# Moving a level-by-level update into places of its own, and running the levels in two groups

## The chip, the cores and the metric

The kernel runs on one core of one Trainium2 chip. The metric is the time of one execution on the device in microseconds (us); the profile comes from one execution of its own. TensorE (PE) multiplies matrices, VectorE (DVE) and ScalarE (ACT) work elementwise, GpSimd (POOL) does a few passes and powers, and SyncE (SP) issues the transfers. Each engine has a queue of instructions in a fixed order and they meet at semaphores. PSUM has eight banks, into which TensorE writes.

## The reference

Two layers run over 2,048 tokens of 256 channels (two sequences of 1,024). Layer 0 is an RWKV block: token shift, five mixed inputs made by a low-rank product, receptance, key, value, gate, a decay of its own for each channel and token, and the recurrence below, then a norm over each head, a gate, an output product; its feed-forward keeps the two largest of four hidden units. Layer 1 is a state-space block and a second feed-forward.

```python
def step(S, inp):                      # one token, each head
    r_t, k_t, v_t, d_t = inp
    kv = k_t[..., :, None] * v_t[..., None, :]
    y = jnp.einsum('bhj,bhji->bhi', r_t, S + u[None, :, :, None] * kv)
    return (d_t[..., None] * S + kv, y)
...
y = (y - mean_of_head) / sqrt(var_of_head + EPS)     # then gamma, beta, times silu(gate)
```

The products of the two branches are multiplied, a SiLU of the feed-forward with the output of the attention, and added to the input.

## The kernel before, in words

The tokens go through in tiles of T = 256. `rounds` calls `one(a, b)` on every engine: `a` is the tile that is in layer 0, `b` the one before it, in layer 1. A first round has only `a`, seven rounds have both (six of them in a hardware loop, one written out), and the last round has only `b`. So the work of two tiles is interleaved by hand in the lists at the end of each engine's `one`. `FILLS` gives for each PSUM bank the names that fill it in turn; `open_bank` waits until the name before was freed, `close_bank` says that a name is filled, `free` is the reader's answer.

**The recurrence** is turned into products. In a tile each pair of blocks of 1, 2, 4, 8, 16, 32 and 64 tokens (`LEVELS`) is a level: the keys of the earlier block, multiplied by the decay up to its end, meet the queries of the later block, multiplied by the decay since its start. `level_update` (L924) multiplies in place, half of `kT` and half of `rT` for each level, so a level can't be multiplied before TensorE has read the level before. TensorE does `own_products` (the tokens with themselves, with the bonus, and level 1), `level(a, 1)` to `level(a, 5)` (blocks 2 to 32) and `level_last` (64). Each level is 16 products of 64x64 tiles, four of which work at once, into one place in the banks L0 and L1 (`lev_pair`); f32 products are two instructions each in the profile. VectorE then takes what counts into `own` with a predicated copy (`level_take`, L938). In the order of TensorE one projection stands between two levels:

```python
first_levels()
ssd_proj(b, "C0", "w_C", 0)
level(a, 1)
ssd_proj(b, "C1", "w_C", 1)
level(a, 2)
gate_in()
```

and so on to `level_last(a)`. `others` (ScalarE) copies the last level out, `last_update` (VectorE) makes the keys and queries for the state, `states_0` the state.

**The gates** are SiLU. ScalarE writes tanh(x/2), VectorE adds one and multiplies by x from PSUM (`hidden`, L860), and a second pass multiplies by the other projection (L864). The same holds for the feed-forward outputs F0 and F1, the gate g and the residual gate. `centred` takes the mean of each head from y (L1089 to L1097), `squares`, `variances`, GpSimd's power and `out_normed` follow.

**The other names.** `next_stats` and `next_normed` (L1054, L1059) normalise the tokens of the next tile; their statistics go to memory and come back as rows (`token_rows`, SP). `differences` makes the input of the rank product. B of layer 1 is turned by VectorE (L1176), stored and loaded again by SP, and multiplied by its decay in `B_decayed` (L1183); `decayed_scores` (L1193) multiplies the scores, `gated_1` (L1211) frees the banks ys0 and ys1, the first of which n1g fills next. GpSimd multiplies C by its decays (L542). `kept_at_work` runs products that nobody reads.

## Time and profile before

| what | value |
|---|---|
| median of three runs | 749.4 us (748.67 to 750.21) |
| the profiled execution | 750.87 us |
| its span, from first to last instruction | 749.1 us |
| TensorE busy | 723.5 us (97%) |
| VectorE busy | 530.1 us (71%) |
| ScalarE busy | 316.9 us (42%) |
| GpSimd busy | 76.2 us (10%) |

Busy time adds up the instructions of an engine without their overlap. The ends of matmuls are modelled, so a busy TensorE can still have slack between instructions. Whoever wants to know what sets the pace in a stretch looks for the engine that doesn't wait there.

### The profile page before, as it was taken

How to read it: one execution, taken by the hardware profiler on the slowest of the kernel's cores; microseconds unless marked ns; L12 is line 12 of the kernel's file. 1: busy time of each engine (PE TensorE's matmuls, PEld its weight loads, DVE VectorE, ACT ScalarE, POOL GpSimd, SP SyncE). 2: the span in 40 equal slices, each digit the busy share in tenths (PEclk: the TensorE clock that was granted, in tenths of full speed). 3: DMA queues.
4: the chain of work that ended last, by engine and by line, in shares of the span. 5: the costliest groups of instructions: out<-in, count | busy, mean ns of one | idle time of the engine just before them, and what ended most of it. 6: DMA issues, size and time to landing. Idle time of an engine off the chain costs nothing.

```text
span 749.1 us, 17781 instructions
## 1 busy us (share of the span) xinstructions
PE 723.5 (97%) x6906; PEld 590.5 (79%) x6906; DVE 530.1 (71%) x1200; ACT 316.9 (42%) x652; POOL 76.2 (10%) x85
## 2 busy tenths in 40 slices
PE   5899999999999999999989999999999999999897
PEld 3777778877888778887778867888778878888686
DVE  3996789836897568956789467984679837896143
ACT  1322583226821466214841058411683236811570
POOL 6201101101011011000110001100101101010020
PEclk9999999999999999999999999999999999999999
DMA  8910451035400363013620145201540036400360
GB/s 277 359 45 0 125 81 27 1 86 142 73 2 11 105 128 58 2 29 101 121 51 2 29 142 86 45 1 44 166 81 10 1 85 142 72 2 14 114 113 16
DMA packets 121597, 55.93 MB, mean 75 GB/s; under 512 B 104305, under 2 KB 113585, under 8 KB 119857
## 3 DMA queue, kind: packets, MB, share of 16 engines
q1 hardware_dynamic: 121520, 54.76, 29.7%
q8 instruction: 66, 1.08, 0.7%
q14 instruction: 11, 0.08, 0.0%
HBM read 42.35 MB, written 12.40 MB: 73 GB/s over the span
## 4 chain that ended last, share of the span: by engine, by line
PE 91%; DVE 5%; issue 2%; ACT 0%; DMA 0%; POOL 0%; DVEq 0%; SPq 0%; ACTq 0%; POOLq 0%
PE psum L1378 71%; PE psum L1480 3%; PE psum L1587 2%; PE psum L1572 2%; PE psum L1451 1%; PE psum L1598 1%; PE psum L1625 1%; PE psum L1793 1%; PE psum L1493 1%; PE psum L1406 1%; PE psum L1440 1%; PE psum L1463 1%; PE psum L1735 1%; PE psum L1672 1%; PE psum L1516 1%
## 5 line engine op out<-in xcount | busy, mean ns | idle before, releaser
L582 ACT ACTIVATE BC<-psum 64x256 f32<-64x256 f32 x128 | 80.9, 632 | 3.5 <-PE psum L1378 1.8
L1378 PE MATMUL psum<-xnT,sb_f_gate 128*128 128x256 f32 x248 | 62.2, 394 | 0.8 <-ACT xnT L595 0.8
L1378 PE MATMUL psum<-xn1T,sb_n_gate 128*128 128x256 f32 x256 | 61.4, 383 | 0.0
L1378 PE MATMUL psum<-xn1T,sb_n_up 128*128 128x256 f32 x256 | 60.5, 379 | 0.0
L1378 PE MATMUL psum<-xnT,sb_f_up 128*128 128x256 f32 x240 | 59.0, 388 | 0.0
L1378 PEld LDWEIGHTS psum<-xn1T,sb_n_up 128*128 128x128 f32 x256 | 48.6, 190 | 6.6
L1378 PEld LDWEIGHTS psum<-xnT,sb_f_gate 128*128 128x128 f32 x248 | 46.7, 194 | 8.5 <-ACT xnT L595 1.2
L1378 PEld LDWEIGHTS psum<-xn1T,sb_n_gate 128*128 128x128 f32 x256 | 47.4, 190 | 6.5
L1378 PEld LDWEIGHTS psum<-xnT,sb_f_up 128*128 128x128 f32 x240 | 43.6, 189 | 7.5 <-DVE S L1075 1.7
L1378 PE MATMUL psum<-sb_f_down,hid 128*128 128x256 f32 x224 | 49.5, 379 | 0.0
L1378 PE MATMUL psum<-sb_n_down,hidB 128*128 128x256 f32 x224 | 49.5, 379 | 0.0
L1378 PEld LDWEIGHTS psum<-sb_f_down,hid 128*128 128x128 f32 x224 | 42.6, 190 | 5.8
L1378 PEld LDWEIGHTS psum<-sb_n_down,hidB 128*128 128x128 f32 x224 | 42.6, 190 | 5.8
L1216 DVE SCALAR_TENSOR_TENSOR thFB<-thFB,psum 128x512 f32<-128x512 f32 x8 | 5.5, 688 | 58.3 <-ACT thFB L707 58.3
L562 ACT ACTIVATE thB<-psum 128x512 f32<-128x512 f32 x32 | 18.8, 592 | 62.8 <-PE psum L1378 62.7
L929 DVE TENSOR_TENSOR kT<-kT,dec 128x256 f32<-128x256 f32 x56 | 23.8, 425 | 30.1 <-PE psum L1480 13.7
L707 ACT ACTIVATE thFB<-psum 128x512 f32<-128x512 f32 x8 | 4.8, 597 | 91.6 <-PE psum L1378 91.6
L534 POOL TENSOR_SCALAR_AFFINE_SELECT cs_row<-cs_row 128x2048 f32<-128x2048 f32 x8 | 16.0, 2004 | 235.9 <-DMA cs_row<-cs_dram 235.9
L608 ACT ACTIVATE cs_row<-cs_row,cs_col 128x128 f32<-128x128 f32 x128 | 38.9, 392 | 0.0
L562 ACT ACTIVATE th<-psum 128x512 f32<-128x512 f32 x32 | 19.0, 593 | 45.5 <-PE psum L1378 37.9
L542 POOL TENSOR_TENSOR cs_half<-cs_half,BC 128x1024 f32<-128x1024 f32 x8 | 19.4, 2421 | 163.7 <-ACT cs_half L674 163.7
L1480 PEld LDWEIGHTS psum<-rT,kT 64*64 64x64 f32 x1280 | 22.3, 134 | 14.0 <-issue 14.0
(216 smaller groups left out, 1515.8 us busy)
## 6 DMA issues: line engine op xcount, KB each, us to landing
cs_row<-cs_dram SPq DMA_DIRECT2D x8, 1024.0 KB, 4.9
x_dram<-gate SPq DMA_DIRECT2D x8, 512.0 KB, 2.8
cs_half<-cs_dram SPq DMA_DIRECT2D x16, 256.0 KB, 5.7
hidB<-x_dram SPq DMA_DIRECT2D x8, 512.0 KB, 5.8
b_dram<-B_turned SPq DMA_DIRECT2D x32, 128.0 KB, 3.2
hidB<-b_dram SPq DMA_DIRECT2D x8, 512.0 KB, 4.3
X<-in_x SPq DMA_DIRECT2D x9, 256.0 KB, 3.5
XT<-in_x_turned SPq DMA_DIRECT2D x8, 256.0 KB, 3.4
```

The source lines that it names most:

```text
L534: g.affine_select(out=cs_row[:, :, :], in_=cs_row[:, :, :], compare_op=ALU.is_ge, fill=NEG, base=0, pattern=[[0, NQ * SCH], [1, P]], chann ...
L542: g.tensor_tensor(cs_half[:, :], cs_half[:, :], BC[:, 1, :, :].rearrange("p t h -> p (t h)"), ALU.mult).then_inc(Cdec_ready, 1)
L562: a_.activation(buf[:, :], ps(t, name + "g")[:, :], ACT.Tanh, scale=0.5).then_inc(ready, 1)
L582: ins = a_.activation(cols[:, par, 2 * pair:2 * pair + 2, :], src[64 * par:64 * par + 64, :, s, :], ACT.Identity)
L608: ins = a_.activation(cs_row[:, n, :], cs_row[:, n, :], ACT.Exp, bias=cs_col[:, n:n + 1])
L929: k_ins = d.tensor_tensor(kk[:, :, 0, :], kk[:, :, 0, :], two[:, :, 1:2].to_broadcast([P, n, s]), ALU.mult)
L1378: ins = t_.matmul(ps(t, name)[first_row:first_row + rows, col:col + n], w, x, start=(k == 0), stop=(k == len(ws) - 1))
L1406: ins = t_.matmul(ps(t, name)[:, i * T:(i + 1) * T], W[w][:, c:c + P], xnT[:, h, 1:T + 1], start=(h == 0), stop=(h == CH - 1))
L1440: ins = t_.transpose(ps(t, name)[:, h * T + q * P:h * T + (q + 1) * P], src[:, q, h * P:(h + 1) * P], ident[:, :])
L1480: ins = t_.matmul(lev_pair[64 * hf:64 * hf + 64, e, g * 32:(g + 1) * 32], flat(kT)[r, n:n + 64], q, start=True, stop=True)
L1572: ins[s] = t_.matmul(ps(t, names[s])[:, i * P:(i + 1) * P], Bf[r, c * P:(c + 1) * P], Cf[r, c * P:(c + 1) * P], start=True, stop=True)
L1587: t_.matmul(y_out(t, s, c, par), Xrow[:, s, c, :], m[:, par, :], start=(c == 0), stop=(c == 0), skip_group_check=True)
```

## The change

Behind the first round, `level_next` takes the place of the update in place: level n reads its keys and queries from place n and writes both halves, the multiplied one and a copy of the other, to place n+1, so VectorE can run ahead of TensorE. The places are buffers whose content is no longer needed at that time. TensorE runs levels 2 to 16 in one group (`low_levels`), each into a quarter of L0 and L1, and 32 and 64 in another (`high_levels`), into a new pair of fills M0 and M1 of the same banks, which opens only when VectorE has taken the low group. Level 1 stays with the own products.

```diff
-FILLS = [["mix_w", "dw", "w0", "k", "mix_g0", "L0", "k0T", "p3g", "F0"],
+FILLS = [["mix_w", "dw", "w0", "k", "mix_g0", "L0", "M0", "k0T", "p3g", "F0"],
...
+        keys_of = [flat(kT), flat(mixed["w"]), flat(mixed["k"]), thF[:, :], thB[0][:, :], flat(xn)]
+        queries_of = [flat(rT), flat(mixed["r"]), flat(mixed["v"]), thB[1][:, :], xn1_turned[:, :], thFB[:, :]]
...
+            def level_next(t, n):
+                s, count = LEVELS[n], CH * T // (2 * LEVELS[n])
+                two = block_decay(s).rearrange("p (b two) -> p b two", two=2)
+                to = (n + 1) % len(keys_of)
+                if n:
+                    dve.wait_ge(lev_ready, t.count(6, n))
+                    dve.sem_inc(passed, 1)
+                for late, place in ((0, keys_of), (1, queries_of)):
+                    x, y_ = halves(place[n], s), halves(place[to], s)
+                    did(d.tensor_tensor(y_[:, :, late, :], x[:, :, late, :],
+                                        two[:, :, 1 - late:2 - late].to_broadcast([P, count, s]), ALU.mult))
+                    ins = d.tensor_copy(y_[:, :, 1 - late, :], x[:, :, 1 - late, :])
+                    if late == 0:
+                        did(ins)
+                ins.then_inc(lev_ready, 1)
...
+            def low_levels(t):
+                for e in range(2):
+                    open_bank(t, f"L{e}")
+                    pe.sem_inc(passed, 1)
+                for n in range(1, 5):
+                    pe.wait_ge(lev_ready, t.count(6, n))
+                    pe.sem_inc(passed, 1)
+                    ins = level_products(LEVELS[n], keys_of[n], queries_of[n], (n - 1) * CH * NQ * 32)
+                for e in range(2):
+                    close_bank(ins[e], t, f"L{e}")
+
+            def high_levels(t):
+                for e in range(2):
+                    open_bank(t, f"M{e}")
+                    pe.sem_inc(passed, 1)
+                pe.wait_ge(lev_ready, t.count(6, 5))
+                pe.sem_inc(passed, 1)
+                level_products(LEVELS[5], keys_of[5], queries_of[5], CH * NQ * 64)
+                level_last(t)
```

The order of VectorE in a steady round becomes:

```diff
-                    next_stats()
                     dve.wait_ge(dec_ready, a.count(1, 1))
-                    level_step(a, 0)
-                    own_keys(a)
-                    level_step(a, 1)
-                    sparse_compare(a, 0, 0)
-                    level_step(a, 2)
...
+                    for n in range(4):
+                        level_next(a, n)
+                    own_taken(a)
                     end_args()
                     B_by_block(0)
...
                     B_by_block(1)
...
+                    level_next(a, 4)
+                    level_next(a, 5)
+                    low_taken(a)
                     gate_0()
+                    sparse_compare(a, 0, 0)
+                    high_taken(a)
                     last_update(a)
                     res_gate(0)
                     res_gate(1)
-                    sparse_count()
-                    hidden_p(a, 2)
+                    sparse_compare(a, 0, 1)
+                    sparse_compare(a, 0, 2)
                     states_0()
                     B_decayed()
                     decayed_scores(0)
+                    hidden_p(a, 2)
                     decayed_scores(2)
                     hidden_p(a, 3)
                     decayed_scores(1)
                     decayed_scores(3)
                     states_1()
+                    sparse_count()
                     sparse_select(0)
                     compare(1)
                     gated_1()
                     sparse_count()
                     sparse_select(1)
-                    centred()
+                    next_stats()
+                    gathered()
```

and TensorE's:

```diff
                     first_levels()
                     ssd_proj(b, "C0", "w_C", 0)
-                    level(a, 1)
                     ssd_proj(b, "C1", "w_C", 1)
-                    level(a, 2)
+                    low_levels(a)
                     gate_in()
-                    level(a, 3)
                     ssd_proj(b, "res0", "w_res", 0)
-                    level(a, 4)
                     ssd_proj(b, "res1", "w_res", 1)
-                    level(a, 5)
                     project_p(a, 2, "u")
-                    level_last(a)
+                    high_levels(a)
                     project_p(a, 2, "g")
```

Beside it the diff holds these parts:

- One-pass gates. Where `whole` is true (p0, p3 and all of n0 to n3 in steady rounds; p2 and p3 in the first), ScalarE writes the SiLU itself and frees the gate's bank, and `hidden` is one pass, `2 * silu * up`. F0, F1 and, in the first round, the gate g are done that way too. `exp_tables` is an Exp of one element a row behind the p0 gate, whose result nobody reads. The other gates stay as they were.
- `weights_centred` (first round, VectorE) takes each head's mean out of the weights of the values, in place. `centred` becomes `gathered`, which only adds Y1 to y.
- `receptances` makes `rU` first and `rT` last; the own products wait for `rU_ready`, the level updates for `rT` and v.
- `next_normed` moves behind `normed_1`, `token_rows` on SP behind the transfers of B, and GpSimd's power for the tokens behind its product of C.
- First round: the weights are loaded in smaller parts and another order, TensorE does half of the p0 gate, the rank product, the other half and the mixes, then p0's up projection; `kept_at_work` goes from 7 and 6 products to 1, 1 and 6.
- Last round: ScalarE keeps `x1_kept` until behind the first copy of X, and the result is made and stored in two halves:

```diff
+                    if b.last:
+                        for q in range(NQ):
+                            half, name = slice(q * C, (q + 1) * C), f"s1{'ab'[q]}"
+                            wait_filled(dve, b, name)
+                            free(d.tensor_tensor(thFB[:, half], thFB[:, half], ps(b, name)[:, 0:C], ALU.mult), b, name)
```

## Rows read from the trace of the kernel before

**Rows 1.** Windows: span, busy by engine, TensorE's clock, DMA.

```profile
200.00:290.00 90.00, 89.70 (x867) 73.61 (x864) 66.00 (x150) 39.89 (x83) 7.40 (x5) 1.00 0.28 63
...
380.00:470.00 90.00, 87.62 (x853) 71.60 (x851) 66.28 (x145) 38.61 (x79) 7.56 (x5) 1.00 0.28 63
```

**Rows 2.** TensorE's waits: total us, times, longest.

```profile
PE psum L1493 <- issue: 1.6, 6, 0.3
```

**Rows 3.** Timeline, TensorE, a steady round: start, length, engine and line.

```profile
263.29 1.89 PE L1378 MATMUL psum<-xnT,sb_f_gate 128*128 128x256 f32 x8
265.02 1.89 PE L1378 MATMUL psum<-mixed_k,sb_w_rkvgo 128*128 128x256 f32 x8
...
274.01 1.99 PE L1378 MATMUL psum<-xn1T,sb_w_C 128*128 128x256 f32 x8
275.93 0.67 PE L1480 MATMUL psum<-rT,kT 64*64 64x32 f32 x32
276.53 1.99 PE L1378 MATMUL psum<-xn1T,sb_w_C 128*128 128x256 f32 x8
```

**Rows 4.** Timeline, VectorE, the same round.

```profile
262.46 0.43 DVE L915 TENSOR_SCALAR dec<-dec 128x512 f32<-128x512 f32 x1 [0.17 <-ACT dec L647]
...
274.42 0.43 DVE L929 TENSOR_TENSOR kT<-kT,dec 128x256 f32<-128x256 f32 x1 [1.36 <-PE psum L1493]
...
275.10 0.72 DVE L936 COPY_PREDICATED own<-masks,psum 128x256 f32<-128x256 int8 x1
...
282.72 0.70 DVE L1176 STREAM_TRANSPOSE B_turned<-BC 128x512 f32<-128x512 f32 x1
```

**Rows 5.** Timeline behind the last level: VectorE, TensorE, GpSimd; last row another round.

```profile
202.11 0.42 DVE L999 TENSOR_TENSOR wins<-beats 128x512 bf16<-128x512 bf16 x1
...
203.47 0.69 PE L1735 MATMUL psum<-v,mixed_w 128*64 128x64 f32 x16
...
204.89 0.97 DVE L1075 SCALAR_TENSOR_TENSOR S<-S,dec,psum 128x64 f32<-128x64 f32 x4
...
205.78 1.15 DVE L1183 TENSOR_TENSOR hidB<-hidB,to_end 128x448 f32<-128x448 f32 x2
...
206.92 2.37 POOL L542 TENSOR_TENSOR cs_half<-cs_half,BC 128x1024 f32<-128x1024 f32 x1 [22.62 <-ACT cs_half L674]
...
215.87 1.28 DVE L1211 TENSOR_TENSOR gate<-gate,psum 128x512 f32<-128x512 f32 x2
...
218.08 1.89 PE L1378 MATMUL psum<-xn1T,sb_n_gate 128*128 128x256 f32 x8
...
384.97 3.32 DVE L1183 TENSOR_TENSOR hidB<-hidB,to_end 128x448 f32<-128x448 f32 x2 [0.73 <-DMA hidB<-b_dram]
```

**Rows 6.** Timeline, ScalarE: p3's gate, and a table load in softplus.

```profile
206.56 0.58 ACT L562 ACTIVATE th<-psum 128x512 f32<-128x512 f32 x1
...
255.53 1.28 ACT L634 ACT_TABLE_LOAD   x1
256.83 0.21 ACT L634 ACTIVATE sp<-sp 128x16 f32<-128x16 f32 x1
```

**Rows 7.** Timeline, TensorE, the first round: p0g, rank product, mixes.

```profile
9.28 3.78 PE L1378 MATMUL psum<-xnT,sb_f_gate 128*128 128x256 f32 x8 [0.75 <-ACT xnT L595]
12.85 1.30 PE L1625 MATMUL psum<-mixed_w,sb_w_mix 128*128 128x256 f32 x4
...
16.57 1.15 PE L1451 MATMUL psum<-aT,sb_w_mix2a 32*128 32x256 f32 x16
```

**Rows 8.** The chain that ended last, first round.

```profile
51.61 0.69 DVE xnT L1059
...
55.98 0.70 DVE gsum L1093
...
57.60 1.34 DVE hid L1016 x4
```

**Rows 9.** Timeline, TensorE, the last round: the transpose of the steps.

```profile
700.53 0.24 PE L1641 MATMUL psum<-ident,aT_dtT 64*128 64x64 f32 x1 [1.55 <-ACT aT_dtT L621]
```

More of the change, by code:

```diff
@@ L300, in build_block, with whole @@
         block = ctx.enter_context(nc.Block())
+        def whole(t, name):
+            return name not in ("p0", "p1", "p2") or (name == "p2" and t.first) or (name == "p0" and not t.first)
         class Steps:
@@ L544, in one @@
                 if a:
+                    rsqrt(a.count(3, 2), token_stats[:, :, 1])
                     rsqrt(a.count(3, 3), head_rstd[:, :], head_var, NQ * HEADS)
@@ L965, in level_step, with own_taken, low_taken, high_taken @@
                 level_take(n).then_inc(lev_ready, 1)
+            def own_taken(t):
+                for e in range(2):
+                    wait_filled(dve, t, f"D{e}")
+                    dve.sem_inc(passed, 1)
+                did(level_take_0(t))
+                after()
+                own_copied(t)
+                for e in range(2):
+                    wait_freed(dve, t, f"D{e}")
+                    dve.sem_inc(passed, 1)
+            def low_taken(t):
+                for e in range(2):
+                    wait_filled(dve, t, f"L{e}")
+                    dve.sem_inc(passed, 1)
+                for n in range(1, 4):
+                    did(level_take(n, None, (n - 1) * CH * NQ * 32))
+                    after()
+                for e in range(2):
+                    free(level_take(4, e, 3 * CH * NQ * 32), t, f"L{e}")
+            def high_taken(t):
+                for e in range(2):
+                    wait_freed(dve, t, f"L{e}")
+                    dve.sem_inc(passed, 1)
+                    wait_filled(dve, t, f"M{e}")
+                    dve.sem_inc(passed, 1)
+                level_take(5, None, CH * NQ * 64).then_inc(lev_taken, 1)
             def own_keys(t):
                 after()
+                own_copied(t)
+            def own_copied(t):
                 for e in range(2):
@@ L1214, in result @@
                 def result():
-                    dve.wait_ge(thFB_ready, b.count(1, 1))
-                    free(d.scalar_tensor_tensor(out=thFB[:, :], in0=thFB[:, :], scalar=1.0, in1=ps(b, "F1")[:, :],
-                                                op0=ALU.add, op1=ALU.mult), b, "F1")
                     wait_freed(dve, b, "F1")
+                    if b.last:
+                        for q in range(NQ):
+                            half, name = slice(q * C, (q + 1) * C), f"s1{'ab'[q]}"
+                            wait_filled(dve, b, name)
+                            free(d.tensor_tensor(thFB[:, half], thFB[:, half], ps(b, name)[:, 0:C], ALU.mult), b, name)
+                            wait_freed(dve, b, name)
+                            d.scalar_tensor_tensor(out=thFB[:, half], in0=thFB[:, half], scalar=0.5, in1=x1_prev[:, q, :],
+                                                   op0=ALU.mult, op1=ALU.add).then_inc(out_ready, 1)
+                        return
                     wait_filled(dve, b, "s1")
@@ L1291, in one @@
                     state_kept()
+                    weights_centred()
                     mix_scaled(a, "w")
@@ L1740, in outputs @@
                     wait_freed(pe, a, "kv")
-                    wait_freed(pe, a, "L0")
-                    wait_freed(pe, a, "L1")
+                    for e in range(2):
+                        wait_freed(pe, a, f"{'L' if a.first else 'M'}{e}")
                     pe.wait_ge(q0_ready, a.count(1, 1))
@@ L1945, in one @@
                     ffn_1(b, hid)
-                    out_1()
+                    wait_freed(pe, b, "ys0")
+                    wait_freed(pe, b, "ys1")
+                    for q in range(NQ):
+                        project(b, f"s1{'ab'[q]}", [(0, P, [gate[:, m, q * P:(q + 1) * P] for m in range(SH // 2)],
+                                                    [W["w_sout"][:, m * C:(m + 1) * C] for m in range(SH // 2)])])
             for f in freed:
```

216 lines of the change are left out of this document (129 added, 87 removed).

## The prediction, made before the change was run

> **What bounds the kernel now.** I read the busy time by stage first [rows 1]. The reader is to see that TensorE works 89.70 of the 90 us of a stretch of steady rounds, so that nothing taken from another engine gives time back there by itself: a steady round gets shorter only by what TensorE itself does or waits for. The second row holds one round in which 2.1 us more of it were lost. The list of TensorE's waits [rows 2] has one entry that comes back in most rounds: six waits at L1493, the own products, of 1.6 us together. The timeline of a round then says what TensorE's own time is made of [rows 3], and the chain and the timelines of the first and last rounds [rows 7 to 9] show where another engine sets the pace.
>
> **Steady rounds, what TensorE gains.** Two projections behind one another start 265.02 - 263.29 = 1.73 us apart. One that has 64x64 products on both sides takes 275.93 - 274.01 = 1.92, so each entry into such a group and each way out of it costs about 0.095. A level itself takes 276.53 - 275.93 = 0.60, though its 32 instructions start within 0.67 - 0.22 = 0.45 (0.22 us is the length of the last): a pitch of 14.5 ns, 0.465 for 32 [rows 3]. So a level that joins another leaves out 0.60 - 0.465 = 0.135 in its group and 0.19 at its neighbours, 0.325. Before, a round has seven groups (own products, five levels, last level), behind the change three (own, 2 to 16, 32 with 64): 4 x 0.325 = 1.30 us. No join is in the trace; the bounds are 4 x 0.19 = 0.76 (each level still drains) and 4 x 0.60 = 2.4 less the products that must stay, that is 1.6. I take 1.30. The own products now wait for `rU` and not for the copy `rT` behind it: the wait of 1.6 / 6, of which I count 0.25, goes [rows 2]. Sum: -1.55 a round.
>
> **Steady rounds, what VectorE must still reach.** Every level update now writes into new places, and the half that isn't multiplied is copied: 12 more instructions of 256 elements. A multiplication costs 0.43, 0.34 from start to start (rows at 274.42 and 275.10, with one more between them); the only one-source instruction over SBUF, 512 elements at 262.46, also takes 0.43, so it runs at two elements a cycle, and a copy of 256 would take 0.30, some 0.22 from start to start [rows 4]. The other bounds are 0.34 (no faster than a multiplication) and 0.63 (the 0.72 of the predicated copy over runs of one element). I take 0.22, since a copy too has one source. The Trainium skill (VectorE: DVE Perf Modes, the perf-mode tier table) gives f32 copies in SBUF twice the rate of two-source instructions; by it the estimate stays 0.22. A level is then 2 x 0.34 + 2 x 0.22 + 0.1 for the wait on itself = 1.23. VectorE was free at 273.06 (274.42 less 1.36 of idling). It no longer waits for the own products, only for ScalarE's copies of r and v, which were done before those products began; four levels from 273.06 end at 278.0. TensorE starts C0 at 273.76 (274.01 less the 0.25), needs 1.82 for it and 1.82 for C1 (one switch each), opens the group at 277.4 and its fourth level at 278.8: no wait. Then come the takes of the own scores (0.72 and twice 0.4), the end arguments (0.5), two turns of B (0.64 each), levels 4 and 5 (2.46) and the takes of four levels, which free the banks (2.2): 286.0. TensorE, behind the group (2.0) and gate, res0, res1 and the up projection (4 x 1.73 and two switches), asks for the banks at 286.5. Cover: 0.5 us. At 0.34 for a copy it is gone, 12 x 0.12 - 0.5 = 0.9 us of waiting a round.
>
> Behind the high levels VectorE does `high_taken` (0.34) and two comparisons (0.95) that used to lie earlier, while the count and `hidden_p(a, 2)` go behind the states. It was busy from 202.11 to 204.89 with those two (2.78) and began the states 0.73 after their bank was filled (203.47 + 0.69 = 204.16). Now it waits for that bank and begins at 204.25, 0.64 sooner. From there to `gated_1` it had 215.87 - 204.89; it gets 2.78 more, 0.12 for one more wait and 0.71 less for the one-pass `hidden_p(a, 3)`: 217.42, and the first half frees its bank 0.66 later, at 218.08. TensorE wants that bank for n1g at 218.08 [rows 5]. A tie: I charge 0.1 a round; the bounds are 0 and 0.7. So 7 x (-1.55 + 0.1) = **-10.15 us**.
>
> The round of [rows 1, 5] that lost 2.1: B arrived 0.73 late, `B_decayed` (1.15 in other rounds) fell on GpSimd's product of 2.37 us, took 3.32 and held up TensorE. Behind the change it begins up to 0.65 sooner, and even 0.73 late ends by 206.9, as that product begins (206.92). I count -2.1 and +0.7 for the wait itself: **-1.4**.
>
> **The one-pass gates.** VectorE loses eight passes of 0.7 in a steady round, under TensorE, so nothing more than I counted. ScalarE gets Silu. If that lies in another table set than Exp, each change costs a load of 1.28, and the next instruction starts 1.30 behind its start [rows 6]. The one that could show is ahead of p3: 206.56 + 1.28 + 0.60 = 208.4, and VectorE asks 4.5 us (states, B, one score, both passes of p2, another score) behind 204.25, at 208.7. Nothing. The Trainium skill (ScalarE: Activation LUTs, What ACT_TABLE_LOAD costs) adds a drain of about 1.38 us to each load; this case's trace shows none in front of the next instruction, and by the page p3 would be about 1.2 us late each round. In the first steady round the explicit Exp sits between the p0 gate and the rank tanh with nothing to hide it: 1.28 + 0.2 less some slack, **+0.6**, once [rows 6]. The normalisation of the next tokens moves behind `normed_1`, and its two transfers on SP behind B's; TensorE asks for it only behind F1, the longest group of projections, which covers it; were that cover gone, it is 1.5 us a round.
>
> **First round.** The rank product moves between the halves of p0g. It ran at 12.85, the mixes at 16.57 [rows 7]; now half of p0g, which takes 3.57 from 9.28 on, and the up projection are out of the way. Estimated from these rows, with the slow pace (3.78 for what takes 1.89 later) up to 13: half of p0g ends at 11.1, the rank products at 13.6, the tanh 14.2, the other half 14.6; mixes at 14.65, **-1.9**. From there VectorE sets the pace, and the weights for it are asked for in the order in which they are wanted. `weights_centred` (1.8 us) lies before the mixes, in VectorE's idle time, if 256 KB land by 14. Later the centring of y (55.98 to 57.60, 1.62) and the two passes at 51.61 (0.69 each, 1.45 with their small one) leave the chain that leads to the output norm, 3.07 in all, of which I leave 0.6 for the wait for Y0's copy, which then comes last: **-2.5**; and one-pass p3 ahead of the last update gives **-0.3** [rows 8]. The filler products go from 13 to 8 and lie in waits: 0.
>
> **Last round.** The transpose of the steps waited 1.55 for ScalarE, which kept x1 first [rows 9]; that copy moves away: **-1.5**. The result goes in two halves: two passes over 256 instead of 512 behind the last product (2 x (0.69 - 0.43)) and half of the bytes in the last transfer, which I put at 0.3: **-0.85**.
>
> **Sum.** -10.15 - 1.4 + 0.6 - 1.9 - 2.5 - 0.3 - 1.5 - 0.85 = -18.0. The profiled execution took 750.87 (its span was 749.1), 1.5 above the median of the three runs; 750.87 - 18.0 = 732.9. I predict **733 us**.
>
> **Rivals.** (a) Copies at 0.34: 0.9 a round, 6 us: 739. For it: nothing shows a copy; against it: 262.46. (b) The Silu switch costs a load and as much again, so that p3 is late and, with VectorE tied to TensorE, TensorE too: 7 x 1.2 = 8.4: 741. Against it: [rows 6]. (c) B's transfer late in most rounds, or the tie of 218.08 is lost by its full 0.7: +5: 738. (d) The first round's gain doesn't come, since weights land later and what VectorE does is unchanged up to the first level: +4: 737. (e) The joins do nothing (0.76 in place of 1.30): +3.8: 737. (f) The other side: the copies over short runs cost as the predicated one, 0.63 from start to start. Then low and high groups together wait 12 x 0.41 - 0.5 = 4.4 a round, 31 us: 763. It decides from (18.0 / 7 + 0.5) / 12 = 0.26 above my 0.22, that is from 0.48 each. For it: predicated copies are slower over single elements [rows 4]; against: multiplications are not.
>
> **Chances.** Forecast 0.45, (a) 0.13, (b) 0.08, (c) and (d) 0.08 each, (e) 0.05, (f) 0.07, better than 728 (TensorE's switches dearer than I count) 0.06. (a) to (e) lie between 737 and 741; two together reach 743. The range 727 to 743 leaves out (f) and some of the tails, 0.2. By itself the forecast has 730 to 736. Within 0.2% (1.5 us, about what a measurement here can tell) lies hardly anything: 0.03; slower 0.08, faster 0.89.
>
> **What the profile will show.** Right: steady rounds 1.4 us shorter; L1480's five groups become two, with 128 products within some 2.0 us; no wait at L1493; n1g and the high levels with waits under 0.2; a one-source pass of 256 elements at 0.30. Wrong: TensorE waits on `own` (L943) or on the gate product, copies of 0.42 or more, `hidden_p(a, 3)` waiting for ScalarE, or mixes of the first round still behind 16 us.

## The result, and the profile of the changed kernel

The changed kernel takes **741.89 us** (median of four executions, 740.68 to 742.74), the kernel before, run beside it on the same chip, 749.81 (748.67 to 751.72). The ratio is 0.9894, with a 95% interval of 0.9873 to 0.9915: faster by 1.1%, 8 us, where the prediction had 16. The profiled execution took 740.68 with a span of 738.9, against 750.87 and 749.1.

The stretches that answer to [rows 1]: windows of the changed kernel, with span, busy time by engine, TensorE's clock, DMA.

```profile
200.00:290.00 90.00, 89.37 (x881) 74.07 (x880) 62.56 (x153) 43.73 (x90) 7.40 (x5) 1.00 0.27 63
380.00:470.00 90.00, 89.38 (x869) 73.78 (x867) 63.34 (x153) 43.70 (x86) 8.73 (x6) 1.00 0.28 63
```

TensorE is still the engine that is always busy, but not quite as busy as in the first row of [rows 1]: it waits 0.3 us more in 90. The second row has no round with 2 us lost. The list of TensorE's waits says where it waits (total us, times, longest):

```profile
PE psum L1702 <- DVE gate L1262: 2.0, 6, 0.3
PE psum L1623 <- issue: 1.5, 6, 0.3
PE psum L1926 <- issue: 1.3, 1, 1.3
PEld psum L1487 <- DVE gate L1312: 2.7, 7, 0.4
```

The wait at the own products (now L1623), which was to go, is still there with the size it had in [rows 2], and scores(0) (L1702) has a wait of about the same size. The last row is of the weight loads (PEld), which normally begin ahead of their products: in all seven rounds one of them waits 0.4 for `gated_1` (L1312), which frees n1g's bank. A round's timeline on TensorE (start, length, engine and line, and in brackets the idle time before):

```profile
181.49 0.89 PE L1623 MATMUL psum<-rU,kT 64*64 64x96 f32 x32 [0.26 <-issue]
182.31 3.72 PE L1487 MATMUL psum<-xn1T,sb_w_C 128*128 128x256 f32 x16
185.96 0.67 PE L1590 MATMUL psum<-mixed_r,mixed_w 64*64 64x32 f32 x32
186.45 0.65 PE L1590 MATMUL psum<-mixed_v,mixed_k 64*64 64x32 f32 x32
186.91 0.65 PE L1590 MATMUL psum<-thB,thF 64*64 64x32 f32 x32
187.38 0.65 PE L1590 MATMUL psum<-xn_turned,thB 64*64 64x32 f32 x32
187.97 1.99 PE L1487 MATMUL psum<-mixed_g,sb_w_rkvgo 128*128 128x256 f32 x8
...
196.16 2.00 PE L1487 MATMUL psum<-xnT,sb_f_gate 128*128 128x256 f32 x8
198.00 0.60 PE L1854 MATMUL psum<-ident,kT 128*128 128x128 f32 x4
198.93 1.16 PE L1702 MATMUL psum<-BC 64*128 64x128 f32 x16 [0.33 <-DVE gate L1262]
```

The four joined levels start 0.46 to 0.49 apart (185.96, 186.45, 186.91, 187.38), and the gate product follows 2.01 behind the first. From the own products to p2's gate, the stretch that holds all levels, a round takes 196.16 - 181.49 = 14.67; the same stretch took 15.97 before (273.19 to 289.16): 1.30 less, the figure of the prediction. But a steady round, from one w_B product (the first projection for B, `ssd_proj(b, "B0", "w_B", 0)`) to the next, went only from 89.13 to 88.54, 0.6 less. The rest of the round gave 0.7 back: p2's gate to scores(0) takes 0.41 more (2.77 against 2.36), scores(0) to n0g 0.13 less, n0g to the F0 product 0.32 more, F0 to the next w_B 0.10 more (the values that most rounds have). -1.30 + 0.41 - 0.13 + 0.32 + 0.10 = -0.60.

What VectorE does around it, in the same round of the changed kernel:

```profile
181.38 0.43 DVE L982 TENSOR_TENSOR mixed_w<-kT,dec 128x256 f32<-128x256 f32 x1 [1.04 <-ACT rT L683]
181.72 0.29 DVE L984 COPY mixed_w<-kT 128x256 f32<-128x256 f32 x1
181.92 0.42 DVE L982 TENSOR_TENSOR mixed_r<-rT,dec 128x256 f32<-128x256 f32 x1
182.25 0.29 DVE L984 COPY mixed_r<-rT 128x256 f32<-128x256 f32 x1
182.69 0.42 DVE L982 TENSOR_TENSOR mixed_k<-mixed_w,dec 128x256 f32<-128x256 f32 x1
...
196.59 0.44 DVE L1005 COPY_PREDICATED own<-masks,psum 128x256 f32<-128x256 int8 x1 [0.66 <-PE psum L1646]
...
197.59 1.28 DVE L1262 SCALAR_TENSOR_TENSOR gate<-gate,psum 128x512 f32<-128x512 f32 x2
...
200.75 0.98 DVE L1172 SCALAR_TENSOR_TENSOR S<-S,dec,psum 128x64 f32<-128x64 f32 x4 [0.94 <-PE psum L1868]
...
213.92 1.29 DVE L1312 TENSOR_TENSOR gate<-gate,psum 128x512 f32<-128x512 f32 x2
```

A copy of 256 elements takes 0.29 and a level 182.69 - 181.38 = 1.31. The reader is to see the two idle times, 0.66 and 0.94, each *in front of* work that TensorE is about to need: `high_taken` waits for the high levels, and the residual gates that free scores(0)'s bank are queued behind it; they end at 198.87 (197.59 + 1.28), and scores(0) begins at 198.93.

Three places outside the steady rounds. The first round's mixes start at 14.65, but from 46 us on TensorE's clock falls (windows; the clock is the figure behind POOL's):

```profile
46.00:48.00 2.00, 1.31 (x20) 0.96 (x18) 0.96 (x1) 0.89 (x2) 0.00 (x0) 0.78 0.00 0
48.00:50.00 2.00, 2.00 (x5) 1.64 (x6) 1.89 (x7) 0.00 (x0) 0.00 (x0) 0.50 0.00 0
50.00:52.00 2.00, 2.00 (x56) 1.54 (x58) 1.51 (x4) 0.00 (x0) 0.00 (x0) 0.87 0.00 0
```

0.50 is 1.2 GHz. In the last round, the timelines of TensorE and of VectorE have these two rows:

```profile
717.52 1.03 PE L1926 MATMUL psum<-hidB 128*64 128x64 f32 x28 [1.26 <-issue]
```

```profile
716.25 1.16 DVE L1284 TENSOR_TENSOR hidB<-hidB,to_end 128x448 f32<-128x448 f32 x2 [4.28 <-DMA hidB<-b_dram]
```

F1 to the prefix sums takes 13.82 before and 12.44 after (-1.38), the prefix sums to the chunk states 23.35 and 24.66 (+1.31), the last output product's start to the end of the span 7.83 and 6.73 (-1.10).

All stretches of the two profiles together: seven steady rounds (six w_B to w_B and one in pieces) about -4.5; what two disturbed rounds had lost before (91.68 and 89.54 against 89.13), -3.0; the first round -2.5; the first steady round's start +0.95; the last round -1.38 + 1.31 - 1.10. The sum is -10.2, the two profiled executions differ by 10.19. The medians differ by 7.9: the profiled execution of the kernel before was one of its longer ones.

### The profile page after: what moved, and what is told of

The parts are those of the page before. It is cut to its first block, busy times and chain, and to the rows that moved or that the text cites. A ratio compares the mean times of both kernels' runs of the same rounds, so it can differ in the third digit from the quotient of the medians.

```text
span 738.9 us, 17998 instructions
## 1 busy us (share of the span) xinstructions
PE 715.5 (97%) x6896; PEld 588.5 (80%) x6896; DVE 496.8 (67%) x1207; ACT 343.4 (46%) x678; POOL 77.5 (10%) x85
## 4 chain that ended last, share of the span: by engine, by line
PE 90%; DVE 5%; issue 2%; ACT 1%; DMA 0%; POOL 0%; DVEq 0%; ACTq 0%; SPq 0%; POOLq 0%
PE psum L1487 69%; PE psum L1590 3%; PE psum L1702 2%; PE psum L1717 2%; PE psum L1515 1%; PE psum L1560 1%; PE psum L1728 1%; PE psum L1926 1%; DVE gate L1262 1%; PE psum L1755 1%; PE psum L1623 1%; PE psum L1549 1%; PE psum L1868 1%; PE psum L1572 1%; PE psum L1663 1%
## 5 line engine op out<-in xcount | busy, mean ns | idle before, releaser
L1487 PE MATMUL psum<-xnT,sb_f_gate 128*128 128x256 f32 x240 | 58.5, 386 | 0.0
L1487 PEld LDWEIGHTS psum<-xnT,sb_f_gate 128*128 128x128 f32 x240 | 44.2, 189 | 6.8 <-issue 0.2
L1327 DVE TENSOR_TENSOR thFB<-thFB,psum 128x512 f32<-128x512 f32 x7 | 4.8, 689 | 40.8 <-ACT thFB L733 40.8
L1487 PE MATMUL psum<-sb_w_X,xn1T 128*128 128x512 f32 x64 | 31.7, 618 | 0.0
L1085 DVE TENSOR_TENSOR beats<-habs 128x768 bf16<-128x768 f32 (+2 forms) x48 | 30.9, 687 | 0.4 <-ACT habs L589 0.4
L1487 PE MATMUL psum<-xn1T,sb_w_B 128*128 128x256 f32 x128 | 30.9, 385 | 0.3
```

Source lines behind the costliest of these rows:

```text
L1085: did(d.tensor_tensor(beats[:, first:first + count, :], habs[:, i:i + 1, :].to_broadcast([P, count, T]), habs[:, i + 1:4, :], ALU.is_ge))
L1487: ins = t_.matmul(ps(t, name)[first_row:first_row + rows, col:col + n], w, x, start=(k == 0), stop=(k == len(ws) - 1))
```

## The experiments

Each is one edit of the changed kernel, or several together where that is said. The kernels of one group ran on one chip with common runs of the kernel before; those groups are e_res_first to e_split, e_fill to e_all, and the last three. The kernel before had medians of 749.29, 749.21 and 750.14 us in them, and of 749.81 beside the changed kernel, so a difference to 741.89 is uncertain by a microsecond or so. By the intervals of the ratios e_count_early, e_split, e_all, e_fill_more, e_no_exp and e_all_more differ from the changed kernel; for e_res_first, e_own_later, e_fill, e_last and e_two_pass the intervals meet or overlap, and what they show stands in their traces.

| kernel | median us | executions | ratio to before, 95% |
|---|---|---|---|
| changed | 741.89 | 740.68 to 742.74 | 0.9894 [0.9873, 0.9915] |
| e_res_first | 738.45 | 736.60 to 739.88 | 0.9854 [0.9835, 0.9874] |
| e_own_later | 739.93 | 739.32 to 740.61 | 0.9877 [0.9859, 0.9896] |
| e_count_early | 735.67 | 733.50 to 736.36 | 0.9816 [0.9799, 0.9834] |
| e_split | 748.62 | 746.52 to 751.68 | 0.9991 [0.9973, 1.0009] |
| e_fill | 742.27 | 739.50 to 745.04 | 0.9920 [0.9905, 0.9935] |
| e_last | 740.12 | 738.75 to 740.64 | 0.9872 [0.9857, 0.9886] |
| e_two_pass | 742.50 | 739.49 to 744.59 | 0.9903 [0.9883, 0.9922] |
| e_all | 732.05 | 731.35 to 734.41 | 0.9779 [0.9764, 0.9793] |
| e_fill_more | 739.19 | 738.70 to 739.65 | 0.9855 [0.9839, 0.9872] |
| e_no_exp | 749.01 | 746.62 to 749.92 | 0.9978 [0.9966, 0.9989] |
| e_all_more | 733.20 | 731.30 to 733.47 | 0.9765 [0.9749, 0.9782] |

**e_res_first.** VectorE, steady rounds:

```diff
+                    res_gate(0)
                     high_taken(a)
                     last_update(a)
-                    res_gate(0)
                     res_gate(1)
```

> One line moved on VectorE in the steady rounds: the first residual gate (L1262, res0) is taken before the taking of the fifth level instead of behind the last update. Theory: TensorE's scores(0) waits in every steady round (L1702 <- gate L1262, 2.0 us in 6 instructions, 0.33 each) because its bank is freed by the second residual gate, and that gate is queued behind the high group's take, which itself waits 0.66 us for TensorE (196.59). The gate of 0.60 us fits into that idle time, so the second gate ends 0.6 us sooner, the wait of 0.33 goes, 7 rounds give -2.3 us: about 739.5 us (ratio to the changed kernel 0.997). In the trace the row L1702 <- gate L1262 is gone. Rival: the wait only moves on to the key transposes or chunk states, or later to n1g and the F0 product, since VectorE's work up to the states is the same: then the row goes but the time stays within 0.5 us of 741.9.

Measured 738.45, 3.4 us less (739.5 was expected). The row of L1702 is gone from the list of waits and nothing took its place: a round takes 88.16 instead of 88.54, 0.38 less, 2.7 us in seven. The trace bears the theory out: the wait was no tie with something else, and it cost what its row says.

**e_own_later.** TensorE, steady rounds:

```diff
                     ssd_proj(b, "B1", "w_B", 1)
-                    first_levels()
                     ssd_proj(b, "C0", "w_C", 0)
+                    first_levels()
                     ssd_proj(b, "C1", "w_C", 1)
```

> One line moved on TensorE in the steady rounds: C0 is computed before the own products (L1623) instead of behind them. Theory: the own products' wait of 0.26 us is not for the scaled receptances but for the bank: D0 opens where r was, and r is freed by the copy to rT, which this change put last on ScalarE. With C0 (about 0.9 us) ahead of them the bank is free in time and the wait goes: 7 x 0.26 = -1.8 us, about 740.0 us. Rival 1: the own products are needed by VectorE's own_taken so early that the delay returns before the low group (the low group waits for the fourth product of keys and decays or VectorE is late by 0.9 us): then the row is gone, other waits appear, and the time is 741.9 or up to 2 us more. Rival 2: the wait is a fixed cost of changing the form of the products and stays at 0.26 wherever the group stands: time the same, L1623 still shows 0.26.

Measured 739.93, and a round of 88.26 to 88.31 in most. The timeline of this kernel:

```profile
180.55 1.89 PE L1487 MATMUL psum<-xn1T,sb_w_C 128*128 128x256 f32 x8
182.37 0.89 PE L1623 MATMUL psum<-rU,kT 64*64 64x96 f32 x32
183.19 1.99 PE L1487 MATMUL psum<-xn1T,sb_w_C 128*128 128x256 f32 x8
185.12 0.67 PE L1590 MATMUL psum<-mixed_r,mixed_w 64*64 64x32 f32 x32
```

L1623 has no wait in front of it and the group of four levels none either, so VectorE can do without the own scores that long. The wait was one for something that comes a little later, not the cost of the switch (rival 2). What it is for is read from the code and the trace: `FILLS` has "r", "D0" behind one another in one bank. In another round of the changed kernel:

```profile
268.37 0.83 ACT L680 ACTIVATE rU<-psum,sb_vecs 128x256 f32<-128x256 f32 x2
269.09 0.61 ACT L683 ACTIVATE rT<-psum 128x512 f32<-128x512 f32 x1
270.04 0.89 PE L1623 MATMUL psum<-rU,kT 64*64 64x96 f32 x32 [0.26 <-issue]
```

`rU` was written by 269.20, the copy that frees the bank was over at 269.70, TensorE's product before ended at 269.78 and the own products began at 270.04: 0.84 behind `rU`, 0.34 behind the bank. In the kernel before, `rU` was the last reader of "r"; it ended at 272.84 and the own products began at 273.19, 0.35 behind it. The order on ScalarE changed, and the bank came free as late as before. The trace names no releaser here, so the bank is the reading that fits best and isn't shown by itself; the run shows that the wait is no fixed cost and is gone when the own products stand one projection later. A kernel with D0 in another bank was not tried.

**e_count_early.** The edit of e_res_first, and

```diff
+                    sparse_count()
                     states_0()
...
                     states_1()
-                    sparse_count()
                     sparse_select(0)
```

> The edit of the first of these kernels, and the first sparse count (L1096 to L1103, 1.6 us) moved from behind the states of the second network to before states_0, into VectorE's idle time there (0.94 us plus the 0.66 that the first edit frees). Theory: VectorE's path from states_0 to the second network's gating is what makes n1g late (its bank ys0 is freed by L1312 at 213.92+0.69), +0.3 us a round against before; with 1.6 us less work there the wait at n1g goes, and the wait of scores(0) too: 7 x (0.33+0.33) or more, about 736.5 to 738 us. Rival: n1g's start is set by TensorE and ScalarE, not by VectorE: then the result equals the first kernel's (739.5 or 741.9).

Measured 735.67, another 2.8 us below e_res_first and somewhat better than expected, and a round of 87.72 to 87.76 in four of six. VectorE in this kernel:

```profile
198.20 0.97 DVE L1172 SCALAR_TENSOR_TENSOR S<-S,dec,psum 128x64 f32<-128x64 f32 x4
...
209.75 1.29 DVE L1312 TENSOR_TENSOR gate<-gate,psum 128x512 f32<-128x512 f32 x2
```

The states to the second network's gating take 11.55 here and 13.17 in the changed kernel: the 1.6 us of the count lie in the idle time instead. The row of the weight load that waits for L1312 is gone, n0g to the F0 product takes 7.01 instead of 7.33, and F0 to the next w_B 37.14 instead of 37.24, as before the change. So n1g's bank, which `gated_1` frees, was indeed late. The two edits change no instruction; they only give VectorE's idle time of 0.66 + 0.94 to work that was in the way.

**e_split.** TensorE, steady rounds; the levels 2 and 4 in one group, 8 and 16 in another (the function takes the first and last level, not shown):

```diff
-                    low_levels(a)
+                    low_levels(a, 1, 3)
                     gate_in()
+                    low_levels(a, 3, 5)
```

> In the steady rounds the low group (four levels, L1590 x128) is cut in two groups of two, with the gate product between them; nothing else. Theory: each join of two groups of these products is worth 0.325 us (1.30 us for four joins, measured on the stretch from the own products to p2g: 15.97 before, 14.67 after), so one join undone costs 7 x 0.325 = +2.3 us, 744.2 us, with the wait of the second half for the operands possible on top. Rival: the 1.30 us came from elsewhere in that stretch (the in-place waits, the separate places), not from the number of groups: then the time stays at 741.9 within 0.7.

Measured 748.62, 6.7 us more instead of 2.3. The timeline of this kernel shows why:

```profile
182.63 0.89 PE L1625 MATMUL psum<-rU,kT 64*64 64x96 f32 x32 [0.25 <-issue]
...
187.59 0.65 PE L1590 MATMUL psum<-mixed_v,mixed_k 64*64 64x32 f32 x32
188.80 1.99 PE L1487 MATMUL psum<-mixed_g,sb_w_rkvgo 128*128 128x256 f32 x8 [0.56 <-DVE own L1068]
...
198.26 0.92 PE L1487 MATMUL psum<-xnT,sb_f_gate 128*128 128x256 f32 x3
```

The stretch from the own products to p2's gate takes 15.63, against 14.67. Of the 0.96, 0.56 are a new wait: the gate product opens the bank behind D0, now 0.9 us sooner, and VectorE has not yet taken the own scores out of it (seven such waits, 4.2 us). The other 0.40 is put down to the switches of one more group, somewhat over the 0.325 of the prediction. The round is 0.9 to 1.2 longer, about what this stretch shows, and seven of them are the 6.7. The theory on the joins holds, the rival (nothing) falls; the size of the whole was missed because the group was also a cover for the bank.

**e_fill.** TensorE, first round only:

```diff
                     level_last(a)
+                    kept_at_work("yT", 1)
                     keys_turned()
+                    kept_at_work("yT", 1)
                     chunk_states()
```

> First round only: one filler product of 256 columns on TensorE ahead of the turning of the keys (0.63 us of waiting) and one ahead of the chunk states (0.69 us); both lie in waits. Theory: the changed kernel's gain in the first round (4.3 us) is partly lost, because the granted clock falls to 1.2 GHz for some 3 us behind these waits (0.78, 0.50 and 0.87 in the windows 46:48, 48:50, 50:52; the down product took 3.27 instead of 1.99 us), in most executions but not in each (in the profile of the kernel with the early count the clock stayed at 1.00, the waits being the same, and the first B projection of the second round began at 76.61 instead of 78.43). With the fillers the clock stays at 1.00 and the time is 1.3 to 1.8 us less: about 740.3 us. Rival: the fall does not hang on these two waits (it comes from the load before them): clock and time as in the changed kernel, or the fillers are themselves in the way: up to +0.3 us.

Measured 742.27: no gain in the median. But its executions lie in steps, and the mean clock of each tells them apart: 739.50 at clock 1.00; 742.19, 742.26 and 742.28 at 0.998; 744.59 and 745.04 at 0.995. I read them as none, one and two falls (every profile of these kernels with a mean clock of 0.997 or 0.998 holds one), of some 2.5 us each. Two waits filled were not enough; the expectation put the price lower, at 1.3 to 1.8, and had the cure wrong.

**e_fill_more.** The products of e_fill and two more, at two waits of the levels:

```diff
-                    kept_at_work("p2u", 1)
+                    kept_at_work("p2u", 2)
                     level(a, 1)
+                    kept_at_work("p2u", 1)
                     gate_mix()
```

> The kernel with the two fillers, and two more of them in the first round: one ahead of the first level (a wait of 0.37 us at 31.4) and one behind it (0.62 us, for the own scores' bank at 32.4). Theory: in every execution of the changed kernel and its variants each fall of the granted clock lasts some 3.3 us and adds 2.4 us to the time (739.5 with none, about 742.2 with one, 744.8 with two), and one of the two places is right behind these waits (34:40 in two of the profiles, 46:52 in four others). With all four waits filled fewer executions have a fall: median about 740 us, most mean clocks at 1.00. Rival: the falls don't hang on waits of this length; the spread stays 739.5 to 745 with a median of 742, or the extra fillers delay the levels: +0.3 us.

Measured 739.19, within 1 us of one another, mean clocks 1.00, 1.00, 1.00 and 0.999. Windows of this kernel:

```profile
30.00:32.00 2.00, 2.00 (x25) 1.51 (x26) 1.33 (x3) 1.45 (x2) 0.00 (x0) 1.00 1.02 418
32.00:34.00 2.00, 2.00 (x43) 1.47 (x36) 1.97 (x7) 0.00 (x0) 0.00 (x0) 1.00 1.05 426
...
46.00:48.00 2.00, 1.75 (x23) 1.25 (x22) 1.29 (x3) 0.85 (x2) 0.00 (x0) 1.00 0.00 0
```

In the changed kernel TensorE was busy for 1.63 and 1.38 of the two us behind 30 and 32, and for 1.11 and 1.31 behind 44 and 46. With all four waits filled (here and in e_all_more) nine executions of nine ran at 0.999 or 1.00, and of the 52 executions of the kernels with none of the four products, the changed one among them, twelve did. So the falls belong to these waits, and they cost the changed kernel 2.7 us in the median. That TensorE idles there isn't enough for a fall, though: the kernel before was busy for 0.90 and 1.31 of the two us behind 46 and 48, and its profile has 1.00 throughout. The kernel before has falls as well and hardly pays for them: in the same group as e_fill it took 748.04 to 749.91 at clock 1.00 and 749.13 to 750.45 at 0.994 to 0.998.

**e_last.** Last round; TensorE, and VectorE:

```diff
                     ffn_n(b, 2)
-                    states()
                     ffn_n(b, 3)
+                    states()
...
+                    decayed_scores(0)
                     B_decayed()
-                    for n in (0, 2, 1, 3):
+                    for n in (2, 1, 3):
```

> Last round only: TensorE computes n3g and n3u ahead of the chunk states of the second network, and VectorE takes the first decayed scores (which free the bank of n3u) ahead of the decay of B. Theory: of the 2.2 us that the last round gained at its start and end, 1.3 came back between the prefix sums and the states, since B comes back from memory as late as before (4.28 us of VectorE's waiting at L1284, 1.26 of TensorE's at L1926) while all else is earlier; with 3.4 us of products ahead of the states the wait goes: -1.2 us, about 740.7 us. Rival: VectorE's chain from B over the scores to the states S1 sets the end of the round, and what TensorE does not wait at L1926 it waits at L1717 or L1728: the time stays at 741.9.

Measured 740.12. From the w_B product of the last round to the last output product it takes 37.83 (694.28 to 732.11), against 39.07: -1.24, the expected 1.2. The chunk states no longer wait; of the rival, a wait of 0.41 us behind them (L1728, here L1729) is true, and the 37.83 hold it.

**e_two_pass.** The second network's gates as before the change (`whole` is false for n0 to n3 in the steady rounds; the tanh has its semaphore again, not shown):

```diff
+            if name[0] == "n" and not t.last:
+                return False
             return name not in ("p0", "p1", "p2") or (name == "p2" and t.first) or (name == "p0" and not t.first)
```

> The one-pass gates of the second network (n0 to n3) are undone in the steady rounds: Tanh on ScalarE and two passes on VectorE, as before the change; all else as changed. Theory: VectorE's four passes of 0.6 us lie under TensorE's products, where VectorE idles 1.1, 2.56 and 1.66 us behind the centring, and ScalarE is spared a table load or two: the time stays within 1 us of 741.9. Rival: VectorE and ScalarE are close to TensorE there, and the one-pass gates carry some of the gain: 0.3 to 0.6 us a round, 744 to 746 us, with waits at n2g or n3g or at the output product in the trace.

Measured 742.50, 739.49 to 744.59: 0.6 more than the changed kernel, whose ratio of 0.9894 lies inside this one's interval; a round takes 88.56 to 88.90 (e_fill, whose steady rounds are those of the changed kernel, has 88.53 to 88.88). VectorE's four passes lie in idle time, as predicted. In the steady rounds the one-pass gates of the second network are not what made the kernel faster.

**e_no_exp.** The explicit Exp (L737) left out, in the steady rounds and in the last (not shown); its result is not used:

```diff
                     ffn_tanh(a, "p0", th[0], th_ready)
-                    exp_tables()
```

> The explicit Exp that draws the table load forward (in the steady rounds and in the last) is left out; its result is used nowhere. Theory: the load of 1.28 us is issued ahead of the wait of its instruction anyhow, so it is hidden wherever ScalarE waits; leaving out the Exp saves at most its 0.2 us and loses nothing: 741.9 within 0.7. Rival: without it the load falls behind the rank product in every steady round and TensorE's mixes wait for it: 1.3 us less cover, up to 7 x 1.0 = +7 us, 749 us, with a wait at L1560 in the trace.

Measured 749.01, 7.1 us more (6.3 by the ratios): my theory falls, and the rival's size is right while its place isn't. ScalarE, in the changed kernel:

```profile
158.10 0.60 ACT L580 ACTIVATE th<-psum 128x512 f32<-128x512 f32 x1 [1.13 <-PE psum L1487]
158.71 1.28 ACT L737 ACT_TABLE_LOAD   x1
160.01 0.20 ACT L737 ACTIVATE one_exp<-head_reset 128x1 f32<-128x1 f32 x1
161.29 0.38 ACT L633 ACTIVATE aT<-psum 128x256 f32<-128x256 f32 x1 [1.08 <-PE psum L1744]
...
163.60 0.22 ACT L652 ACTIVATE sp<-sp 128x16 f32<-128x16 f32 x1
163.84 1.28 ACT L654 ACT_TABLE_LOAD   x1
```

and without the Exp, with TensorE's wait behind it:

```profile
162.40 0.38 ACT L633 ACTIVATE aT<-psum 128x256 f32<-128x256 f32 x1 [2.60 <-PE psum L1742]
...
164.69 1.28 ACT L652 ACT_TABLE_LOAD   x1
...
166.22 1.28 ACT L654 ACT_TABLE_LOAD   x1
...
169.24 1.28 ACT L658 ACT_TABLE_LOAD   x1
```

```profile
171.04 0.72 PE L1800 MATMUL psum<-decT,sb_dec 64*128 64x128 f32 x8 [0.98 <-ACT decT L658]
```

The tanh at L633 runs without a load behind Silu and behind Exp, so both sets hold it. Without the Exp its load comes only at the softplus (L652), where ScalarE has no slack, and three loads lie one behind the other ahead of the decay's tanh (L658), for which TensorE waits: 0.98 in every steady round. With the explicit Exp the first load lies in an idle time of 2.6 us. In the first steady round it costs as much as it saves: from the rank product to the mixes 0.97 less without it (71.14 to 74.79, against 70.15 to 74.77), and 0.98 of waiting at L1800. The last round loses 1.28 without it: TensorE's wait for the prefix sums (L1485 in this kernel) grows from 0.57 to 1.85:

```profile
701.46 0.38 PE L1485 MATMUL psum<-prefix,before 128*128 128x2 f32 x2 [1.85 <-DVE prefix L1245]
```

Six times 0.98 and 1.28 make 7.2.

**e_all** and **e_all_more**: e_count_early, e_own_later and e_last together, e_all with the two products of e_fill, e_all_more with the four of e_fill_more.

> All edits that took a wait away together: first residual gate early, count early, C0 ahead of the own products, the two fillers of the first round, the order of the last round. Theory: they lie at different places and add up: 6.2 (first two, measured) + 2.0 (own products, measured) + 1.3 (fillers) + 1.2 (last round) under 741.9 = 731.2 us. Rival: VectorE and TensorE are tied, so that TensorE's earlier own products only turn into waits for VectorE's takes or for the count: 733 to 735 us.

> All edits together with the two further fillers. Theory: the kernel with all edits ran in 731.35 to 734.41 us (median 732.05), three of five at clock 1.00; with the further fillers the median is 731.5 to 732 and the slowest execution under 733. Rival: no change in the spread, or +0.3 us for the two products.

Measured 732.05 and 733.20, where 731.2 and 731.5 to 732 were expected: the parts add up less than fully, and the two further fillers brought nothing (slowest execution 733.47, not under 733). A round takes 87.52 to 87.74 in e_all, 0.9 less than in the changed kernel, though the three edits by themselves gave 0.38, 0.44 and 0.27, 1.09: nearly a sum. The last kernel ran at clock 1.00 in all five executions and has the best ratio, 0.9765 [0.9749, 0.9782], but the intervals of the two overlap: they can't be told apart. In its profile the steady rounds take 87.60 to 88.03, and the first begins at 77.86 instead of 76.76, 0.7 of it lost before the mixes of the first round, which start at 15.36 instead of 14.63; why is open. Either beats both kernels, the changed one by 1.2% to 1.3%.

## Why the prediction was right and where it failed

Right, by its own steps. *The joins*: 1.30 a round forecast and measured on the stretch; 0.40 for one of them undone, where 0.325 was taken. Rival (e) is out. *The copies*: 0.29 long and 0.20 from start to start, where 0.30 and 0.22 were taken; rivals (a) and (f) are out. The Trainium skill (VectorE: DVE Perf Modes, the perf-mode tier table) gives f32 copies in SBUF twice the rate of a product of two tensors, and the trace agrees: 512 elements from one source took 0.43 and 256 take 0.29, so 0.14 is for 256 elements and 0.15 fixed, which leaves 0.27 for those of the product of 0.42. *The table load*: the gate behind the load of 202.82 starts at 204.12, 1.30 later, and p3 is in time; rival (b) is out. The Trainium skill (ScalarE: Activation LUTs, What ACT_TABLE_LOAD costs) adds a drain of 1.38 to each, of which neither this row nor the pair 158.71 and 160.01 shows anything. *The last round's transpose*: -1.38 for -1.5; *the halves*: -1.10 for -0.85; *the mixes*: 14.65, to the digit. *The first steady round*: +0.95 for +0.6.

Wrong, with what the runs put in its place:

1. "A tie: I charge 0.1 a round." The steady rounds gave 0.6 each, not 1.45. Two waits stand for most of that. One was not in the sum: `res_gate(1)` frees the bank of scores(0), and the change queues it behind `high_taken`, which waits for TensorE; 0.38 a round, shown by e_res_first. The other is the tie itself, 0.42 at n1g and behind it (e_count_early: 0.44 less), a little over the middle of my 0 to 0.7. VectorE's own path was forecast to the hundredth, 13.17 from the states to `gated_1`; what I left out is that the weight load wants the bank too, and sooner: in the kernel before n1g's load began 0.21 ahead of its product (306.99 and 307.20), in the changed one both begin at 214.66, 0.08 behind the gate that frees the bank. I had followed VectorE's amount of work past these points and not, bank by bank, what each of its instructions frees and who is waiting in front of it.
2. "The own wait ... of which I count 0.25, goes." It stayed at 0.26. I read the semaphore of `rU` and not the bank, which ScalarE frees as late as before, whatever the order of its three instructions (0.35 and 0.34 ahead of the own products). e_own_later takes the wait away, whichever of the two it was for: 0.27 a round, 2 us.
3. "-1.9, -2.5 and -0.3" in the first round, 4.7 together. The engines did nearly what was forecast: in the profile of e_count_early, whose first round is that of the changed kernel and whose clock stayed at 1.00, the first w_B product of the steady rounds starts at 76.61 and not 78.43, and at 79.98 before; without the +0.95 of the first steady round, 4.3 less than before. That the clock could fall was in no term. It falls in most executions, and here it costs: 2.7 us (e_fill_more).
4. In the last round the gain at its start came back at the chunk states, 1.3 us, since B's load was issued 31.5 us behind F1's start (680.42 to 711.96) as against 31.7 before, while TensorE was 1.4 ahead; SP issues B's store (703.90) behind two loads of cs_half whose issue takes 5.07 (4.07 before). e_last hides it.

Items 1 to 4 by the medians: 6.2 + 2.0 + 2.7 + 1.8 = 12.7; all of them together gave 9.8 (e_all, with two of the four fillers) or 8.7 (e_all_more, with four) over the changed kernel. The single differences carry their noise and share some of their gain. e_all ran in 732.05, and the prediction was 733; its steady rounds take 87.52 to 87.74, and 89.13 - 1.45 is 87.68. So the forecast of the steady rounds was that of a kernel in which these waits don't arise; that the whole times also agree is in part luck, since e_all has two further edits, of the first and the last round. The direction and the range held, the size of the gain was put at twice the true one. Of the rivals (c), B late or the tie lost by its full 0.7, was nearest in kind and had 738.

The forecast also was counted from a profiled execution with two disturbed rounds. For the one at 380 us a gain of 1.4 was counted; both went, 3.0 in the profiles; the medians differ by 2.3 less than the profiles do. What made those two rounds longer before was not tried. Nor was the change's level part by itself, without the gates and the new first round.

## What to carry to other kernels

When work moves between engines that meet at shared banks, list for every bank the instruction that frees it and what is now queued in front of that instruction; two of the five losses above, and by the best reading a third, were a bank freed some 0.3 us late, and moving a few lines, with two products that nobody reads, gave 9.8 us where the change had given 7.9. If an engine is idle in front of an instruction that waits for another engine, whatever stands behind it and is ready should go ahead of it. In this kernel a table load was best put where ScalarE is idle, even at the price of an instruction of its own.

## What the runs showed of the hardware

- The granted clock of TensorE fell to 1.2 GHz (0.50) behind waits of 0.3 to 0.7 us that followed one another (busy 1.63 and 1.38, or 1.11 and 1.31, of 2 us), in some executions of one kernel and not in others. It fell at 46 to 52 us in four of the thirteen profiles, at 34 to 40 in three, once in each, and the first w_B product came at 78.2 to 79.8 us in these, at 76.6 to 76.8 in four of the other five changed ones. A fall was worth some 2.5 us of time by the steps of e_fill. With products that nobody reads in the four waits (2.00 and 1.75 of 2 us busy) it stayed at 1.00 in nine executions of nine.
- Silu and Exp lie in separate table sets that both hold Tanh (loads of 1.28 between the two, none at the tanh of L633 behind either). So a kernel has the choice of where the load lies: 7.1 us of 742 for one instruction of 0.20 us a round.
- Joined groups of 32 64x64 products start 0.46 to 0.49 apart, where a single one cost 0.60 and 0.19 in its neighbours.
- A bank freed late delays the weight load as well as the product: the load of n1g began 0.21 us ahead of its product where the bank was free (306.99 and 307.20), and together with it where it wasn't (214.66).
